# A chain of modulated convolutions on one core: the prologue written out per engine, and the builds of the edge weights split into steps

## The reference, cut to what matters

```python
def _layer(x, style, w, b, mw, mb, typ):
    s = style @ mw.T + mb
    weight = SCALE * w * s[:, None, :, None]
    demod = lax.rsqrt(jnp.sum(weight * weight, axis=(2, 3)) + EPS)
    weight = weight * demod[:, :, None, None]
    # same: 3-tap conv + bias;  upsample: transposed conv, stride 2, + bias, then blur
    # downsample: blur, then conv, stride 2, + bias
TYPES = ('same', 'upsample', 'same', 'downsample')
for i, typ in enumerate(TYPES):
    out = _layer(out, style, weights[i], biases[i], mod_w[i], mod_b[i], typ)
x = x + out          # once per block, four blocks
```

## Time and profile before

| | us |
|---|---|
| median of 3 runs | 1465.87 |
| lowest and highest | 1465.85, 1468.49 |
| the profiled execution | 1465.1 |
| its span, first to last instruction | 1463.3 |
| PE busy | 1409.7 (96%) |
| DVE busy | 1022.6 (70%) |
| ACT busy | 701.6 (48%) |
| POOL busy | 377.3 (26%) |

### The profile page before, as it was taken

The page is one execution under the profiler, slowest core; times in us unless marked ns, Lnnn a source line. Parts: engine busy times, 40 slices in busy tenths (PEclk is TensorE's granted clock), DMA queues, the critical chain, the costliest instruction groups (busy, mean ns, idle before and its releaser), DMA issues.

```text
span 1463.3 us, 21189 instructions
## 1 busy us (share of the span) xinstructions
PE 1409.7 (96%) x7436; PEld 1188.8 (81%) x7436; DVE 1022.6 (70%) x1634; ACT 701.6 (48%) x1128; POOL 377.3 (26%) x771
## 2 busy tenths in 40 slices
PE   3799999999999999999999999999999999999998
PEld 3587877877888888888888888888888888888887
DVE  5787787877667667757666766766766776676674
ACT  2444444445544444544554544454565454454454
POOL 3425225143322122131132213112232212212111
PEclk9899999999999999999999999999999999999999
DMA  5000000001340000000053000000032000000004
GB/s 222 6 0 6 1 1 7 1 0 63 89 141 3 1 1 1 1 1 1 1 138 94 1 1 1 1 0 1 1 102 72 1 1 1 1 0 1 1 9 107
DMA packets 20040, 39.65 MB, mean 27 GB/s; under 512 B 1760, under 2 KB 2400, under 8 KB 19936
## 3 DMA queue, kind: packets, MB, share of 16 engines
q1 hardware_dynamic: 19648, 37.68, 8.9%
q10 hardware_dynamic: 288, 0.62, 0.1%
HBM read 21.48 MB, written 16.81 MB: 26 GB/s over the span
## 4 chain that ended last, share of the span: by engine, by line
PE 91%; DVE 6%; issue 1%; ACT 1%; DMA 0%; POOL 0%; ACTq 0%; SPq 0%; DVEq 0%; POOLq 0%
PE ps L355 28%; PE ps L357 27%; PE ps L356 27%; PE ps L361 3%; PE ps L362 3%; PE ps L450 1%; PE ps L468 1%; DVE xl L709 1%; PE ps L460 1%; DVE gl L757 1%; DVE vh L740 1%; DVE vl L741 1%; DVE gl L761 1%; PE ps L440 0%; PE ps L312 0%
## 5 line engine op out<-in xcount | busy, mean ns | idle before, releaser
L543 ACT ACTIVATE zh<-ps,t_bx 128x512 fp32r<-128x512 f32 x256 | 176.4, 689 | 692.4 <-PE ps L357 692.4
L355 PE MATMUL ps<-zh,gh 128*128 128x512 f32 x1024 | 411.5, 402 | 0.0
L357 PE MATMUL ps<-zh,gl 128*128 128x512 f32 x1024 | 404.3, 395 | 0.0
L356 PE MATMUL ps<-zl,gh 128*128 128x512 f32 x1024 | 404.2, 395 | 0.0
L715 DVE SCALAR_TENSOR_TENSOR zl<-ps,t_bx,zh 128x512 fp32r<-128x512 f32 x256 | 190.9, 746 | 97.5 <-ACT zh L543 95.9
L357 PEld LDWEIGHTS ps<-zh,gl 128*128 128x128 f32 x1024 | 194.2, 190 | 46.0
L725 DVE SCALAR_TENSOR_TENSOR X<-ps,t_D,X 128x511 f32<-128x511 f32 x256 | 190.9, 746 | 52.5 <-PE ps L357 52.3
L356 PEld LDWEIGHTS ps<-zl,gh 128*128 128x128 f32 x1024 | 194.0, 189 | 41.3
L355 PE MATMUL ps<-xh,w0h 128*128 128x512 f32 x512 | 207.3, 405 | 20.5 <-DVE xl L709 20.5
L355 PEld LDWEIGHTS ps<-zh,gh 128*128 128x128 f32 x1024 | 193.0, 189 | 41.0
L709 DVE SCALAR_TENSOR_TENSOR xl<-X,t_S,xh 128x513 fp32r<-128x513 f32 x256 | 199.9, 781 | 6.6 <-ACT xh L534 2.4
(11 more groups left out here) (135 smaller groups left out, 2021.7 us busy)
## 6 DMA issues: line engine op xcount, KB each, us to landing
X<-x_in SPq DMA_DIRECT2D x32, 513.0 KB, 6.3
out_x<-X SPq DMA_DIRECT2D x64, 256.5 KB, 3.8
pk<-taps_in SPq DMA_DIRECT2D x4, 512.0 KB, 10.9
pk<-pack_in SPq DMA_DIRECT2D x3, 352.0 KB, 10.6
pk<-sets_in SPq DMA_DIRECT2D x4, 192.0 KB, 2.3
pk<-pack_in ACTq DMA_DIRECT2D x1, 352.0 KB, 3.5
w3f<-w_in ACTq DMA_DIRECT2D x1, 256.0 KB, 5.2
misc<-small_in SPq DMA_DIRECT2D x1, 82.5 KB, 3.3
```

The source lines that it names most:

```text
L355: pe.matmul(out_ap, ah, bh, start=first, stop=False, skip_group_check=True)
L356: pe.matmul(out_ap, ah, bl, start=False, stop=False, skip_group_check=True)
L357: return pe.matmul(out_ap, al, bh, start=False, stop=last, skip_group_check=True)
L543: act.activation(zh[n % 2][:, ZPAD:ZPAD + M], ps[:, ZP + n % 2, :], IDENT, bias=tab["bx"][:, k, b:b + 1]).then_inc(s["zhi"], 1)
```

## The change

The loops of all engines start at n = 0, and what came before is written out by hand for each engine. The weights of block 0 come in pieces, on two queues; `w3f` comes as block 0's part and the rest. Demodulation's reciprocal, root and Newton steps run in three parts (`PARTS`): layer index 2 alone, then 0 and 1, then 3. `w3q` and its low part for quad 0 are made on DVE, two of the three tap products of `rf` and the low parts `w2l`, `w0l`, `rl` of block 0 on POOL. Semaphores that stood for several tiles (`wh`, `wl`, `rt`, `et`, `tabs`) are divided. Newton's step has three instructions instead of four. An ACT Sqrt on a cleared tile stands first on ACT. `build` does one tap per call; its calls lie in slots 0 to 3 for block 0, and in slots 12, 15, 16 and 19 for the others; the `sets` transfer moves from slot 0 to slot 4. The diff, cut to its core (the new functions `w2hi`, `w0hi`, `rhi` of ACT hold lines that stood in `setup`):

```diff
 V_LEAD, G_LEAD = 7, 4
 EDGE_SLOTS = (3, 4, 6, 7)
 PS = 2 * GS
-BUILD_SLOTS = (12, 15)
+PARTS = (slice(2, 3), slice(0, 2), slice(3, 4))
+NPART = len(PARTS)
+BUILD = {12: ((0, 0), (0, 1)), 15: ((0, 2), (1, 0)), 16: ((1, 1),), 19: ((1, 2),)}
+BUILD_FIRST = {0: ((0, 0), (0, 1)), 1: ((0, 2),), 2: ((1, 0), (1, 1)), 3: ((1, 2),)}
 SQUARES, STYLE, DEMOD, NEWTON, TABLES, BIAS_U, BIAS_S, SPLIT_W, R_TAP0, R_TAP1, R_TAP2, SPLIT_R, RECIP = range(13)
 SETUP_SLOTS = {0: (SQUARES, R_TAP0), 1: (STYLE,), 2: (DEMOD,), 3: (RECIP, R_TAP1), 4: (NEWTON,), 6: (R_TAP2,), 7: (TABLES,),
...
-            return (k, SETUP_SLOTS.get(i, ())) if 0 <= n and k < NBLK else (None, ())
+            k, i = n // PS + 1, n % PS
+            return (k, SETUP_SLOTS.get(i, ())) if k < NBLK else (None, ())
         def build_at(n):
-            if n == -1:
-                return 0, (0, 1)
-            k, i = n // PS + 1, n % PS
-            return (k, (BUILD_SLOTS.index(i),)) if n >= 0 and k < NBLK and i in BUILD_SLOTS else (None, ())
+            at = [(0, step) for step in BUILD_FIRST.get(n, ())]
+            return at + [(k, step) for k in range(1, NBLK) for step in BUILD.get(n - (k - 1) * PS, ())]
         def sets_at(n):
-            return n // PS if n >= 0 and n % PS == 0 and n // PS < NBLK else None
-        FIRST = -V_LEAD
+            return n // PS if n >= 0 and n % PS == 4 and n // PS < NBLK else None
...
             sp.dma_start(misc[:, :], small).then_inc(s["c_small"], 16)
-            sp.dma_start(pk[:, 0, PACK:WALL], taps[0]).then_inc(s_taps[0], 16)
-            for b in range(0, 2 * GS, 2):
+            sp.dma_start(pk[0:C, 0, OFF_WT:OFF_W1N], taps[0, 0:C, 0:OFF_W1N - OFF_WT]).then_inc(s["wa"], 16)
+            load(0)
+            sp.dma_start(pk[:, 0, OFF_W0:WALL], taps[0, :, OFF_W0 - PACK:]).then_inc(s["w0f"], 16)
+            sp.dma_start(pk[C:128, 0, OFF_WT:OFF_W1N], taps[0, C:128, 0:OFF_W1N - OFF_WT]).then_inc(s["wb"], 16)
+            sp.dma_start(pk[:, 0, OFF_W1N:OFF_W0], taps[0, :, OFF_W1N - PACK:OFF_W0 - PACK]).then_inc(s["wb"], 16)
+            for b in range(2, 2 * GS, 2):
                 load(b)
+            sp.dma_start(w3f[:, 1:, :, :].rearrange("p k j c -> p (k j c)"), w3in[:, 2 * C:]).then_inc(s["w3rest"], 16)
...
-                    sp.wait_ge(s["et"], k + 1)
+                    sp.wait_ge(s["eto"], k + 1)
...
-                    pe.wait_ge(s["wl"], k + 1)
+                    pe.wait_ge(s["w0l"], k + 1)
...
+                pe.wait_ge(s["w2l"], k + 1)
...
+                pe.wait_ge(s["rl"], k + 1)
...
-                    pe.wait_ge(s["et"], k + 1)
+                    pe.wait_ge(s["ety"], k + 1)
...
+                    pe.wait_ge(s["eto"], k + 1)
...
-            for n in range(FIRST, NN):
-                if 0 < n + 1 < NN or n == -2:
-                    conv0(max(n + 1, 0))
+            v_products(0)
+            conv0(0)
+            g_products(0)
+            conv0(1)
+            setup(0, BIAS_U)
+            v_products(1)
+            setup(0, BIAS_S)
+            pe.wait_ge(s["z0"], 1)
+            for n in range(NN):
+                if n == 0:
+                    convg(n)
+                elif n + 1 < NN:
+                    conv0(n + 1)
...
-                if n >= 0:
+                if n > 0:
...
-            act.dma_start(pk[:, 0, 0:PACK], pack[0]).then_inc(s_pack[0], 16)
-            act.dma_start(w3f[:, :, :, :].rearrange("p k j c -> p (k j c)"), w3in).then_inc(s["w3in"], 16)
+            act.dma_start(pk[:, 0, 0:OFF_W2], pack[0, :, 0:OFF_W2]).then_inc(s_pack[0], 16)
+            act.dma_start(pk[:, 0, OFF_W2:OFF_WT], pack[0, :, OFF_W2:OFF_WT]).then_inc(s["w2f"], 16)
+            act.dma_start(w3f[:, 0, :, :].rearrange("p j c -> p (j c)"), w3in[:, 0:2 * C]).then_inc(s["w3in"], 16)
+            def squares(k):
...
+            def root(l, count):
+                act.wait_ge(s["rcp"], count)
+                act.activation(dall[:, l, :], tmp[:, l, :], ACT.Sqrt).then_inc(s["sqrt"], 1)
...
                     act.wait_ge(s_pack[k], 16)
                     act.wait_ge(s_taps[k], 16)
-                    if k >= 1:
-                        act.wait_ge(s["Dp"], k)
-                        act.activation(wsq[:, 3], w1T[0:C, k], ACT.Square)
-                        act.activation(wsq[:, 0:3], wT[:, k], ACT.Square).then_inc(s["wsq"], 1)
-                    act.activation(w2h[:, k], w2f[:, k], ACT.Copy)
-                    act.activation(w0h[:, k], w0f[:, k], ACT.Copy)
-                    for h in range(2):
-                        ins = act.activation(w2d[h * C:(h + 1) * C, k], w2f[0:C, k], ACT.Copy)
-                    ins.then_inc(s["wh"], 1)
+                    act.wait_ge(s["Dp"], k)
+                    squares(k)
+                    w2hi(k)
+                    w0hi(k)
+                elif stage == RECIP:
+                    root(slice(0, NLAY), k + NPART)
...
-                act.wait_ge(s["bv1"], k + 1)
+                act.wait_ge(s["sq"], k + 1)
...
-                act.wait_ge(s["tabs"], k + 1)
+                act.wait_ge(s["bv2" if k else "bv1"], k + 1)
...
+            act.wait_ge(s["warm"], 1)
+            act.activation(uq[:, :], uq[:, :], ACT.Sqrt)
+            act.wait_ge(s["wa"], 16)
+            squares(0)
+            act.wait_ge(s["w2f"], 16)
+            w2hi(0)
+            root(PARTS[0], 1)
+            rhi(0)
+            act.wait_ge(s["w0f"], 16)
+            w0hi(0)
             w3hi(0)
-            setup(0, SPLIT_W)
-            for n in range(FIRST, NN):
-                if 0 <= n + 2 < NN:
+            xhi(0)
+            root(PARTS[1], 2)
+            root(PARTS[2], 3)
+            vhi(0)
+            xhi(1)
+            act.wait_ge(s["z0"], 1)
+            zhi(0)
+            w3hi(1)
+            ghi(0)
+            ghi(1)
+            vhi(1)
+            for n in range(NN):
...
+            def recip(l, count):
+                dve.wait_ge(s["var"], max(1, count - NPART + 1))
+                dve.reciprocal(tmp[:, l, :], var[:, l, :]).then_inc(s["rcp"], 1)
+            def newton(l, count):
+                dve.wait_ge(s["sqrt"], count)
+                a, b, c = tmp[:, l, :], dall[:, l, :], var[:, l, :]
+                link(dve.scalar_tensor_tensor(a, b, -0.5 * SCALE, b, ALU.mult, ALU.mult))
+                link(dve.tensor_tensor(a, a, c, ALU.mult))
+                link(dve.scalar_tensor_tensor(b, a, 1.5 * SCALE, b, ALU.add, ALU.mult))
...
-                    if k >= 1:
-                        dve.wait_ge(s["wsq"], k)
-                    else:
-                        dve.wait_ge(s_taps[k], 16)
-                        dve.wait_ge(s_pack[k], 16)
-                        dve.tensor_tensor(wsq[:, 0:3], wT[:, k], wT[:, k], ALU.mult)
-                        link(dve.tensor_tensor(wsq[:, 3], w1T[0:C, k], w1T[0:C, k], ALU.mult))
+                    dve.wait_ge(s["wsq"], k + 1)
                     link(dve.tensor_tensor(wsum, wsq[:, :, 0, :], wsq[:, :, 1, :], ALU.add))
-                    link(dve.tensor_tensor(wsum, wsum, wsq[:, :, 2, :], ALU.add))
+                    dve.tensor_tensor(wsum, wsum, wsq[:, :, 2, :], ALU.add).then_inc(s["ws"], 1)
...
+                    dve.tensor_copy(T["S0"], sall[:, 0, :])
...
-                    dve.wait_ge(s["var"], k + 1)
-                    dve.reciprocal(tmp, var).then_inc(s["rcp"], 1)
+                    recip(slice(0, NLAY), k + NPART)
...
+                    newton(slice(0, NLAY), k + NPART)
+                    dve.tensor_tensor(T["E2"], sall[:, 3, :], dall[:, 2, :], ALU.mult).then_inc(s["e2"], 1)
...
+                    link(dve.tensor_tensor(T["bz"], tmp[:, 0, :], ch(bi[0]), ALU.mult))
...
-            for stage in (SQUARES, STYLE, R_TAP0, DEMOD, RECIP, SPLIT_W, R_TAP1, NEWTON, TABLES, R_TAP2, SPLIT_R):
-                setup(0, stage)
-            dve.wait_ge(s["z0"], 1)
...
+            def w3first():
...
+                e = tab["E2"][:, 0, 0:QS].unsqueeze(1).unsqueeze(3).broadcast_to([128, 2, QS, C])
+                w = w3f[:, 0, :, :].unsqueeze(2).broadcast_to([128, 2, QS, C])
+                dve.tensor_tensor(w3q[:, :, :, :], w, e, ALU.mult).then_inc(s["w3q"], 1)
...
+            def w3first_low():
...
+            def rsum_first():
+                dve.wait_ge(s["rp"], 2)
...
+                    ins = dve.tensor_tensor(rf[0], rf[0], rp[i], ALU.add)
...
+                ins.then_inc(s["rf"], 1)
+            setup(0, R_TAP0)
+            setup(0, STYLE)
+            setup(0, SQUARES)
+            rsum_first()
+            setup(0, DEMOD)
+            recip(PARTS[0], 1)
+            newton(PARTS[0], 1)
+            dve.tensor_tensor(tab["E2"][:, 0, :], sall[:, 3, :], dall[:, 2, :], ALU.mult).then_inc(s["e2"], 1)
+            w3first()
+            setup(0, SPLIT_W)
+            w3first_low()
+            xlo(0)
+            link(dve.tensor_tensor(tab["E1"][:, 0, :], sall[:, 2, :], sall[:, 1, :], ALU.mult))
+            recip(PARTS[1], 2)
+            recip(PARTS[2], 2)
+            vfull(0)
```

(131 more changed lines are left out.)

89 lines of the change are left out of this document (51 added, 38 removed).

## The result

The changed kernel takes 1442.23 us (median of 4 runs, 1441.61 to 1443.26) against 1466.29 before; the ratio is 0.9834, with a 95% interval of 0.9817 to 0.9851. That is 24.1 us less, by the medians. The profiled execution is one of 1441.61 us, with a span of 1439.8, 23.5 less than before.

What follows compares the result with a forecast made beforehand. TensorE, busy 96%, was taken as the bound, so only its 53.6 us without matmul could be won by reordering; 1465.1 minus 20.7 (prologue) minus 3.5 (hand-overs) gave 1441 us, range 1434 to 1452.

Steps and rivals of the forecast that it cites:

- steps 1 and 2: Prologue, start and third layer alone: v products at 13.4 us instead of 22.49, with ACT ending last.
- step 3: Prologue, v to g: stays 5.59 us, g at 19.0; conv0(0) fits inside as free work.
- step 4: Prologue, DVE's work from 19.0 us, 1 us allowed for POOL's `w3lo(1)`: convg(0) at 28.5 instead of 56.29.
- step 5: Prologue: g of quad 1 behind convg(0), at about 33.5 us; conv0(4) then at 47.6.
- the 2 us that the prediction worked out from the Trainium skill: Prologue: POOL's products beside DVE would make the sum some 2 us higher, by the rule on shared SBUF interfaces.
- step 6: Block 0's builds in n = 0 to 3: 2 us come out as waits; conv0(4) at 49.6, 20.7 earlier.
- step 7: Block hand-overs, builds divided 3, 3, 2, 2: 3.5 of 6.9 us of `xl` waits saved; `rdl` waits stay 5.6.
- PE's idle time in all about 30 us: Whole kernel: a sign that the forecast is right, beside v near 13.4, convg(0) near 28.5, conv0(4) near 50.
- The builds didn't eat the start: Rival, n = 0 to 4: all 7.4 us of builds on the path, nothing won at hand-overs; 1450 us, chance 0.2.
- The clock stayed at 1.00: Rival, prologue: clock stays low; convg(0), g of quad 1, conv0(2) cost 2.3 + 2.3 + 1.3; 1447 us, chance 0.12.
- The start did not end on a transfer: Rival, prologue: the chain ends on a transfer, ACT delayed to 14, giving 2 to 3 us back; 1444, chance 0.08.
- The slower case: Rival, slots 15 to 19: POOL falls behind, PE waits for `w3l` or `eto`; 1470 us, chance 0.02.

Runs made afterwards that it cites:

- the run with one part: The changed kernel with block 0's reciprocal, root and Newton steps over all four layers at once: 1443.05 us.
- the run with tiny builds: The changed kernel with every build operation on 8 columns of the 512, for all blocks: 1434.34 us.
- weights whole: The changed kernel with block 0's weights in whole transfers again, taps ahead of all loads of x, pack and w3 on ACT's queue: 1444.41 us.

## Why the prediction was right

1441 was forecast and 1442.2 measured; 24.2 us of gain on the profile, and 23.5 found. The place and the cause were right: the prologue, shortened by a new order of the chain, with the builds moved behind it. That the sum came so near is partly luck, in two places: inside the prologue, and between the prologue and the hand-overs. Point by point:

- Start to v (steps 1 and 2): 13.4 forecast, 14.18 measured. What I left out was the stretching of DVE's operations beside POOL: the pair of `w2dl` took 1.28 us (0.84 in the kernel before), and the copy of `S0` 0.69 for 0.2. The copy was made up for by the style products, which began at 3.97 and not 4.4. That ACT, not DVE, would end last before `w3h` fell out differently: both arrived at 12.1, and then DVE's stretched `w2dl` came last.
- v to g and the free conv (step 3): 5.6 forecast, 6.03 measured. The conv inside is free: with it moved out, g stands 6.03 us behind v as well. The 0.4 us more are DVE's: beside POOL's `rl` the product for `E1` took 1.18 us for some 0.2, the reciprocals behind it ran to 17.29, and `vf` began at 17.21, when the last v product had ended at 16.68. Moving the conv out costs 4.1 us.
- convg(0) at 28.5 (step 4): 28.43, by luck. DVE came to `gp` at 24.85 where the sum had 23.9, 0.95 us late. The sum then had 1 us for POOL's `w3lo(1)` beside the `gl` operations; it ended at 26.21, before they began at 26.77, and they took 0.69, 0.42 and 0.35 us, unstretched. The two errors cancelled. That DVE's sum of work sets convg(0), and not the chain to v, is shown by the run with one part, which moved v by 2.2 us and convg(0) by 1.0 only.
- g of quad 1 at 33.5 (step 5): 33.53. The 1.1 us that the sum had for hand-overs and POOL's gather and `w3q` went mostly into one operation: `vl` took 1.43 us beside `w3q`, for 0.69.
- So the 2 us that the prediction worked out from the Trainium skill ("GPSIMD Engine Reference", section Engine selection) for POOL's work beside DVE did not show in the sum: 0.8 at v, 0.95 at `gp` (not all of it from POOL), nothing at convg(0), where 1 us was already allowed.
- Builds in n = 0 to 3 (step 6): I took 2 us of waits ahead of conv0(4), which comes at 47.73 where the sum without them gave 47.6. The waits lie behind it (0.54 and 0.72 us) and are worth 1.4 by the run with tiny builds. This is why the prologue brought 22.6 us at conv0(4) and not 20.7.
- Hand-overs (step 7): the term that was wrong. Forecast 3.5 us off the waits for `xl`, found 2.4; and the words "with three in the row DVE falls behind by half" name a wrong cause. The first wait of a hand-over stayed at 1.6 us with three operations behind v as with five. Slots 14 and 15 differ by where POOL waits for v; with the steps ahead of it the wait is gone, and fives begun in slot 14 left 1.7 us of 6.9. The waits for `rdl` stayed at 5.5, as forecast.
- The sign "PE's idle time in all about 30 us" did not come: it is 34.2. The sum took the whole gain for idle time, and 4.1 us of it are products no longer run at the lower clock.
- The rivals. The builds didn't eat the start. The clock stayed at 1.00 in the profile of the changed kernel; in four of the profiles above (one part, conv0(0) behind g, weights whole, tiny builds) it fell at the place named, behind convg(0), but cost 1.2 to 1.5 us between g of quad 1 and conv0(2), instead of 6. The start did not end on a transfer: ACT began its squares at 5.23, and `w0h` and `w3h` followed without a wait for a transfer. The slower case did not show: PE never waited for `w3l` or `eto` in the loop.

The two larger errors, 1.9 us too little in the prologue and 2.6 too much behind it, partly cancelled.

## What to carry to other kernels

Where one engine's waits are the bound, follow the queue of the engine that ends last to the yardstick, with durations from the trace; here that gave the new prologue within 2 us at every milestone (convg(0) fits within 0.1 only because two errors cancelled, and g of quad 1 is counted from it), and the run that removes one part tells what that part is worth (the conv in the gap 4, the demodulation in parts 1). Work of a helper engine that stretches another's instructions should be put by phase: look in the timeline for where the helper engine waits for the same event as the busy one, and put the work ahead of that wait in its queue, not behind it. Work moved between slots of an engine that is full in all of them only moves the wait; sum each slot before moving.
